# A two-layer attention kernel: feed-forward values held in PSUM from gate product to rounding, and the rounding offset made by two ScalarE passes

## The reference, cut to what matters

```python
def fp4_quant_dequant(x):                      # blocks of 16 along the last dim
    scale = max(abs(block)) / 6.0, at least 1e-12
    xn = xb / scale
    idx = searchsorted([0.25, 0.75, 1.25, 1.75, 2.5, 3.5, 5.0], abs(xn))
    q = [0, 0.5, 1, 1.5, 2, 3, 4, 6][idx] * sign(xn) * scale
def fp4_linear(x, w):
    return einsum('bsk,nk->bsn', fp4_quant_dequant(x), fp4_quant_dequant(w))
gate = fp4_linear(x, w_gate)                   # 128 -> 352
y = fp4_linear(x, w_up)
h = silu(gate) * y
return fp4_linear(h, w_down)                   # 352 -> 128, x is the layer-normalised input
```

## Time and profile before

| | us |
|---|---|
| median of 3 runs | 913.84 |
| lowest and highest of them | 913.34, 918.64 |
| the profiled execution, its own time | 913.45 |
| its span in the profile | 911.7 |
| first feed-forward step, first block maxima of x to last residual | 383.1 to 546.3 |
| second feed-forward step, the same | 745.4 to 909.0 |

### The profile page before, as it was taken

How to read it: one execution, slowest core, us unless ns; L and a number is a source line. 1 busy time by engine, 2 the same in 40 slices (tenths; PEclk the granted TensorE clock), 3 DMA queues, 4 the chain that set the end, 5 groups by cost and what they waited for, 6 DMA issues and landing times.

```text
span 911.7 us, 14036 instructions
## 1 busy us (share of the span) xinstructions
PE 639.3 (70%) x5231; PEld 464.9 (51%) x5231; DVE 584.0 (64%) x1062; ACT 300.4 (33%) x507; POOL 354.6 (39%) x423
## 2 busy tenths in 40 slices
PE   2458878887665777755766654899988965666575
PEld 1457756666333346734544442465555533554454
DVE  7525553331795985668988752566676657878863
ACT  2221113332242332044444321333333334444332
POOL 6620000000000001446777675255565444666664
PEclk9568999999897888968898966788999997889886
DMA  9300000000000000000000000000000000000001
GB/s 257 78 1 1 1 0 1 1 0 1 2 0 1 1 0 1 1 1 0 1 0 1 0 1 0 1 1 2 1 2 1 2 2 0 1 13 23 12 12 35
DMA packets 13676, 10.47 MB, mean 11 GB/s; under 512 B 1399, under 2 KB 12599, under 8 KB 13493
## 3 DMA queue, kind: packets, MB, share of 16 engines
q1 hardware_dynamic: 13620, 9.73, 3.8%
HBM read 7.63 MB, written 2.10 MB: 11 GB/s over the span
## 4 chain that ended last, share of the span: by engine, by line
PE 48%; DVE 23%; POOL 13%; issue 10%; ACT 5%; ACTq 0%; DMA 0%; DVEq 0%; POOLq 0%
PE ps L1052 5%; PE ps L1138 4%; PE ps L1270 4%; PE ps L1206 3%; PE ps L1167 3%; PE ps L1079 3%; PE ps L1188 3%; POOL arena L268 3%; PE ps L1289 2%; POOL arena L265 2%; DVE r L770 2%; POOL arena L258 2%; PE ps L1197 2%; DVE arena L845 2%; DVE hblk L818 2%
## 5 line engine op out<-in xcount | busy, mean ns | idle before, releaser
L1188 PE MATMUL ps<-wguT,arena 128*128 128x352 f32 x128 | 61.9, 572 | 34.5 <-DVE arena L845 33.1
L320 POOL TENSOR_TENSOR ln<-mv,lnc 128x4 f32<-128x4 f32 x64 | 13.6, 213 | 154.7 <-DVE mv L650 154.7
L339 POOL MEMSET early<- 128x2560 f32 x2 | 4.5, 2231 | 172.3 <-PE ps L1123 161.6
L1138 PE MATMUL ps<-G,xw 128*126 128x512 f32 x72 | 46.6, 800 | 30.0 <-ACT xw L492 22.3
L1180 PE MATMUL ps<-eye,arena 128*128 128x128 f32 x64 | 15.3, 383 | 73.7 <-POOL arena L258 65.3
L368 POOL TENSOR_SCALAR_AFFINE_SELECT arena<-arena 128x1024 f32<-128x1024 f32 x32 | 35.0, 1093 | 80.6 <-ACT arena L607 80.6
L1206 PEld LDWEIGHTS ps<-wdT,arena 128*128 128x128 f32 (+1 forms) x384 | 57.7, 226 | 15.2 <-ACT arena L546 7.6
L1206 PE MATMUL ps<-wdT,arena 128*128 128x128 f32 (+1 forms) x384 | 58.4, 311 | 5.4 <-ACT arena L546 5.4
L268 POOL TENSOR_TENSOR arena<-arena,hblk 128x704 f32<-128x704 f32 x32 | 60.1, 1880 | 2.5
L1189 PE MATMUL ps<-wguT,arena 128*128 128x352 f32 x128 | 57.1, 532 | 0.0
L931 DVE TENSOR_TENSOR arena<-ps,tri 128x1024 f32<-128x1024 f32 x32 | 39.2, 1224 | 27.2 <-PE ps L1270 27.2
(11 more groups left out here) (193 smaller groups left out, 1627.9 us busy)
## 6 DMA issues: line engine op xcount, KB each, us to landing
X<-in_x SPq DMA_DIRECT2D x8, 256.0 KB, 4.7
out<-X SPq DMA_DIRECT2D x8, 256.0 KB, 2.3
wqkv<-in_wqkv SPq DMA_DIRECT2D x1, 1024.0 KB
band<-in_band SPq DMA_DIRECT2D x1, 897.8 KB
early<-in_wfc SPq DMA_DIRECT2D x1, 512.0 KB
kI<-in_scaled_eye SPq DMA_DIRECT2D x1, 192.0 KB
wattn<-in_wattn SPq DMA_DIRECT2D x1, 192.0 KB, 7.5
S<-in_wd SPq DMA_DIRECT2D x1, 176.0 KB, 3.5
```

What stands on the lines that cost most here:

```text
L1138: last = mm(ps[0:WI, w, :], xw[:, w * WO:w * WO + WI], G1[:, b, :], start=True, stop=True)
L1188: mm(ps[:, 2 * k, 0:F], x, wguT[:, 0:F], start=True, stop=True).then_inc(s["f_gate"], 1)
```

## The change

The change does the following.

- h never goes to SBUF. Up lies in banks 1 and 2 for even pairs and 3 and 4 for odd ones (`up_banks`); `gated` multiplies in place, the maxima read there, the ratio is written there, and `move_h` reads there. All gate products share bank 0 (`GATE_BANK`), so a tile's gate waits for silu of the tile before.
- `normalise` writes x to PSUM bank 7 (`X_BANK`), where maxima and ratio work in place. That bank holds one quad, so normalise(q+1) waits until x(q) plus offset is done, where before it waited for the ratio.
- The offset is made by two ACT passes, `Square` (of 704 or 512 columns from PSUM, to bf16) and `Identity` with a bias of 2^22 * 4/3, in place of ACT's absolute value and DVE's clamp.
- Transposes of x and of h share bank 5 (`T_BANK`), and the second tile's transposes of h share bank 6 with down. `hT_copy` is two copies of 384 columns. For p = 1, DVE adds down from PSUM to X (`residual`), and neither `down_copy` nor POOL's residual is there.
- PE's `x_transposes` and ACT's `xT_copy` stand ahead of `gate_up(2r+3)` and `silu(2r+3)`. ACT's first `normalise` of p = 1 waits for the end of the linear attention.

```diff
+GATE_BANK, X_BANK, T_BANK = 0, 7, 5
+SQ = (RND / 6.0) ** 0.5
...
+            for k, c in enumerate((1e-5, -0.5, -1.0, RND * 4.0 / 3.0)):
...
-                    if 0 <= r - 3 < PN:
+                    if p == 0 and 0 <= r - 3 < PN:
                         residual(r - 3)
...
-                    need(a, "fx_ratio", n)
+                    need(a, "fx_moved", n)
...
+                def offset_h(r):
+                    n = ffn_pairs(p, r)
+                    a.wait_ge(s["fh_ratio"], n + 1)
+                    need(a, "fh_offset", n)
+                    act(hsquare[:, :].rearrange("p (k n) -> p k n", k=2), up_banks(r), ACT.Square, scale=SQ).then_inc(s["fh_square"], 1)
+                    a.wait_ge(s["fh_square"], n + 1)
+                    need(a, "fh_grid", n - 1)
+                    act(hoff[r % 2][:, :], hsquare[:, :], ACT.Identity, bias=lnc[:, 3:4]).then_inc(s["fh_offset"], 1)
...
                     if 0 <= r + 1 < PN:
                         silu(2 * r + 2)
-                    if 0 <= r - 2 < PN:
+                    if 0 <= r - 2 < PN and p == 0:
                         down_copy(r - 2)
+                    if r % 2 and q < QN:
+                        xT_copy(q)
                     if 0 <= r + 1 < PN:
                         silu(2 * r + 3)
                     if 0 <= r < PN:
-                        absolute("fh", hratio, hoff[r % 2], ffn_pairs(p, r), ffn_pairs(p, r) - 1)
+                        offset_h(r)
...
                         normalise(q + 1)
-                    if r % 2 and q < QN:
-                        xT_copy(q)
...
+                    up = up_banks(t // 2)[:, t % 2, :]
+                    tt(out=up, in0=up, in1=sil[t % 2], op=ALU.mult).then_inc(s["f_h"], 1)
...
+                def residual(r):
+                    v.wait_ge(s["f_down"], ffn_pairs(p, r + 1))
+                    tt(out=X[:, 2 * r:2 * r + 2, :], in0=ps[:, T_BANK + 1, 0:2 * P].rearrange("p (k c) -> p k c", k=2),
+                       in1=X[:, 2 * r:2 * r + 2, :], op=ALU.add).then_inc(s["f_x_done"], 1)
...
+                    need(pe, "f_silu", n)
+                    mm(ps[:, GATE_BANK, 0:F], x, wguT[:, 0:F], start=True, stop=True).then_inc(s["f_gate"], 1)
+                    need(pe, "fh_moved", ffn_pairs(p, max(r - 1, 0)))
+                    mm(up_banks(r)[:, t % 2, :], x, wguT[:, F:2 * F], start=True, stop=True).then_inc(s["f_up"], 1)
...
                         down_mms(r - 2)
+                    if r % 2 and q < QN:
+                        x_transposes(q, r)
                     if 0 <= r + 1 < PN:
                         gate_up(2 * r + 3)
-                    if r % 2 and q < QN:
-                        x_transposes(q)
                     if 0 <= r - 1 < PN:
                         h_transposes(r - 1)
```

More of the change, by code:

```diff
@@ L81, in build @@
         ln = sb("ln", [P, 4, TILES])
-        lnc = sb("lnc", [P, 3])
+        lnc = sb("lnc", [P, 4])
         rstd, shift = ln[:, 1, :], ln[:, 3, :]
@@ L102, in build @@
         used[0] = 0
-        xin, xratio, xmoved, xgrid = (part(QD * P) for _ in range(4))
+        xmoved, xgrid = (part(QD * P) for _ in range(2))
         xquant = part(QD * P).rearrange("p (k c) -> p k c", k=QD)
@@ L106, in build @@
         sil = [part(F) for _ in range(2)]
-        h, hratio, hgrid = (part(2 * F) for _ in range(3))
+        hgrid = part(2 * F)
         hmoved = [part(2 * F) for _ in range(2)]
@@ L551, in down_copy, with offset_x @@
                     need(a, "f_x_done", n - 1)
[L552 to L557, removed]
+                    act(down[r % 2], ps[:, T_BANK + 1, 0:2 * P].rearrange("p (k c) -> p k c", k=2), ACT.Copy).then_inc(s["f_down_copied"], 1)
+                def offset_x(q):
+                    n = ffn_quads(p, q)
+                    a.wait_ge(s["fx_ratio"], n + 1)
+                    need(a, "fx_offset", n)
+                    act(xsquare[:, :], ps[:, X_BANK, :], ACT.Square, scale=SQ).then_inc(s["fx_square"], 1)
+                    a.wait_ge(s["fx_square"], n + 1)
+                    need(a, "fx_grid", n)
+                    act(xoff[:, :], xsquare[:, :], ACT.Identity, bias=lnc[:, 3:4]).then_inc(s["fx_offset"], 1)
+                def offset_h(r):
[6 more added lines that the diff above has]
+                    act(hoff[r % 2][:, :], hsquare[:, :], ACT.Identity, bias=lnc[:, 3:4]).then_inc(s["fh_offset"], 1)
+                if p == 1:
+                    a.wait_ge(s["lin_x_done"], TILES)
                 normalise(0)
@@ L843, in gated, with absmax_h @@
                     v.wait_ge(s["f_up"], n + 1)
[L844 to L848, removed]
+                    up = up_banks(t // 2)[:, t % 2, :]
+                    tt(out=up, in0=up, in1=sil[t % 2], op=ALU.mult).then_inc(s["f_h"], 1)
+                def absmax_h(r):
+                    v.wait_ge(s["f_h"], ffn_tiles(p, 2 * r + 2))
+                    reduce(out=pair(hblk[r % 2][:, 0, :]), in_=blocks(up_banks(r)), axis=AX, op=ALU.max,
+                           apply_absolute_value=True).then_inc(s["fh_absmax"], 1)
@@ L862, in ffn @@
+                    if r % 2 == 0 and q < QN:
+                        absmax_x(q)
+                    if r % 2 and q < QN:
+                        move_x(q)
+                    if p == 1 and 0 <= r - 2 < PN:
+                        residual(r - 2)
+                    if 0 <= r < PN:
+                        inverse("fh", hblk[r % 2], ffn_pairs(p, r))
+                        ratio_h(r)
+                    if r % 2 == 0 and q < QN:
+                        ratio_x(q)
                     if p == 0 and 0 <= r - 4 < PN:
@@ L865, in ffn @@
                         tile_stats(2, 2 * r - 7)
[L866 to L878, removed]
+                    if 0 <= r < PN:
+                        move_h(r)
             ffn(0)
```

114 lines of the change are left out of this document (65 added, 49 removed).

## The result

| | before | after |
|---|---|---|
| median of four runs, us | 914.25 (913.34 to 918.64) | 943.01 (937.33 to 946.10) |
| the profiled execution's span | 911.7 | 944.4 |

The changed kernel is slower: ratio 1.0299, 95% interval 1.0242 to 1.0356. The forecast was 944.0, range 928 to 962.

A forecast was written before the change was run, and what follows sets the result against it. The prediction took a loop through several engines, with DVE close behind, as the bound. Per step 15.0 - 7.9 + 8.0 = 15.1, both 30.2, on 913.45 gave 943.7 and a median of 944; range 928 to 962.

The forecast's parts named there:

- Odd iterations: Feed-forward iterations in which x is rounded: gate and silu wait behind POOL's x, 13.0 us against 8.4 today.
- Even iterations: Feed-forward iterations between the odd ones: shorter way from ratio to addition, 7.5 us in place of 9.5 and more.
- 0.2 for DVE's residual: Even iterations: DVE's residual of p = 1 lies mostly under the wait for the scales and adds 0.2 us.
- The fill: First scale of x to gated of tile 1: 19.9 us where it was 12.0, 8.0 more per step.
- The new wait for the end of the linear attention: ACT's first normalise delayed by about 1 us, costed at nothing because POOL's first scale comes later anyway.
- Iterations without x and the tail: Iterations 12 to 14 at 6.35 us each save 5.9, the last iteration and behind it 2.0: -7.9 per step.
- rival C: Dearer: POOL's multiplies stay at 1.91 and 1.58, 957 us; or down at half clock in even iterations, 951; over 955: 0.16.
- A: Faster: contention goes and DVE's loop sets the pace everywhere, if x's transposes finish early; 850 us, chance 0.06.
- B: PE stays at 2.4 GHz, so transposes and gate save 0.9 per odd iteration: 932 us, chance 0.10.
- D: A wash: losses and gains cancel, needing odd iterations of 10.5 or less; about 915 us, chance 0.04.

The follow-up runs named there:

- e6: The changed kernel with x's transposes and their copy one iteration later, between down and gate of the even iteration: 854.0 us, ratio 0.9334.
- e8: The changed kernel with seven unused 128x352 matmuls on PE ahead of the wait for x in odd iterations 1 to 11: 933.9 us, ratio 1.0224.
- e3: The changed kernel with only ACT's copy of x moved behind silu(2r+3), ahead of the offset of h; PE as changed: 946.4 us, ratio 1.0335.
- e10: e6 with POOL making h's scale ahead of x's in even iterations and DVE's residual behind the ratio of h: 849.7 us, ratio 0.9305.
- e1: The changed kernel with PE's transposes of x and ACT's copy of x back at their places of before: 916.1 us, ratio 1.0018.
- e9: The kernel before with only x's transposes and their copy moved to the even iteration behind POOL's rounding of x: 901.6 us, ratio 0.9859.
- e5: The changed kernel with ACT's absolute value and DVE's clamp in place of Square and Identity: 936.2 us, ratio 1.0254.

## Why the prediction was right

**Odd iterations: 13.0 predicted, 12.95 measured.** Term by term in iteration 5 of the second step: start to scale 2.04 (2.03); to the subtraction 0.44 (0.43); to the multiply 1.59 (1.60); to PE's transposes 7.76 from the start (7.8); to gate 0.90 (0.86); to silu 1.42 (1.41); silu 0.36 (0.46); Square 0.78 and Identity 0.92 with their handovers (0.84 each); addition 0.81 (0.81). e6 shows that this order is what cost it: with nothing but the place moved, 12.95 becomes 6.34 to 7.65.

**Even iterations: 7.5 predicted, 7.33 and 7.38 measured.** Of the 0.2 for DVE's residual only 0.05 was there, the difference between the two steps: in iteration 6 it runs from 847.79 to 848.21, and the scale of h, for which the reciprocal waits anyway, is done at 848.04. Iterations 1 to 11 came to 114.4 per step instead of 115.5, +13.9 and not +15.0.

**The fill: +8.0 predicted, +8.0 measured** in both steps, and by the way that was laid out: in the second, x(0) takes from its scale at 764.47 to the transposes at 770.50 (6.0, predicted 5.9), normalise(1) starts at 772.12 behind the copy, and x(1) takes 6.0 again (774.61 to 780.58). The new wait for the end of the linear attention was put at nothing; POOL's first scale waited 0.18 us for the maxima behind it.

**Iterations without x and the tail: -7.9 per step predicted, -5.1 and -6.7 measured.** This is the mis-sized term. I gave all three iterations 6.35. Iterations 12 and 14 took 6.34 in the first step and 6.61 in the second, but iteration 13 took 7.74 and 8.25. So the three saved 4.0 and 3.6 and not 5.9. (In the first step they took 24.4 in the kernel before, where the prediction took 25.0 over from the second.) The last iteration and what is behind it saved 1.1 and 3.1 where I had 2.0 for both. Iteration 13 in the second step:

```profile
912.20 1.38 PE L1235 MATMUL ps<-wguT,arena 128*128 128x352 f32 x2
...
914.55 1.66 PE L1256 MATMUL ps<-wdT,arena 128*128 128x128 f32 x12
...
916.24 0.42 DVE L900 TENSOR_TENSOR X<-ps,X 128x256 f32<-128x256 f32 x1 [2.13 <-PE ps L1256]
...
916.58 0.42 DVE L848 RECIPROCAL hblk<-hblk 128x44 f32<-128x44 f32 x1
```

PE comes out of a thin stretch at half clock (gate and up 1.38 each), so down is late, DVE's residual waits for it for 2.13 us, and the reciprocal of h stands behind the residual although its scale was ready at 914.63. That is close to the mechanism that I had as half of rival C, and put into the even iterations instead; but down itself takes 1.66 here, and it is late because gate and up ran at half clock ahead of it. The first step has no residual on DVE. There gate and up take 1.36 and 1.38, down 2.03, and the gate behind them holds the silu that Square stands behind, 1.4 us after the ratio is done:

```profile
538.32 2.03 PE L1256 MATMUL ps<-wdT,arena 128*128 128x128 f32 x12
...
539.00 0.90 DVE L888 SCALAR_TENSOR_TENSOR ps<-ps,hblk 128x704 f32<-128x704 f32 x1
...
540.98 0.46 ACT L547 ACTIVATE arena<-ps 128x352 f32<-128x352 f32 x1 [0.21 <-PE ps L1235]
541.34 0.75 ACT L576 ACTIVATE hsquare<-ps 128x704 bf16<-128x704 f32 x1
```

In e8, where PE had been kept busy up to iteration 11, iteration 13 took 6.35 and 6.61, with gates of 0.76 in the second step. It is not there every time: e3, without that, took 7.73 and 6.61. So the term had left out that PE can come into an iteration without x at half clock.

**The sum.** Per step +13.9 + 8.0 - 5.9 = 16.0 against 15.1 predicted; the stages outside gave +0.6 net. The profiled execution took 946.1 instead of 943.7 and the median 943.0 instead of 944. The closeness of the last figure is in part luck: errors of opposite sign (-2.2 in the iterations, +4.0 in the tails), and a profiled execution that was the slowest of four between 937.3 and 946.1.

**The rivals.** *A* (850): the time of its world exists, e6 and e10, but needs the place that the change doesn't have; that condition was named. *B* (full clock): half clock was there, gate 1.38, and costs what B said, as e8 shows, 933.9 against B's 932. *C*: POOL's multiplies stayed at 1.38 and 1.06 throughout, so its first half is refuted; down took 1.60 in even iteration 6, so its second half did not come true where it was put. *D* (a wash) needed x two POOL instructions earlier; e1 gives 916 by another way, by moving the loss between iterations.

**The rule on DVE's fixed cost.** The Trainium skill (VectorE: DVE Perf Modes, section on the TRN2 errata) has a fixed cost that is 62 cycles higher for a PSUM source than for an SBUF one. The trace doesn't agree: the addition of h, with a PSUM source and its result in SBUF, takes 0.89 us, and the undisturbed one, all in SBUF, took 0.89 too. The ratio, PSUM to PSUM, takes 0.899 where the undisturbed one in SBUF took 0.89.

## What to carry to other kernels

When an edit shortens instructions on two busy engines, first find whom the last wait of the loop names; if it is a queue position on a third engine, the gain doesn't arrive until that position is changed too (here -1.4% for the place alone, +0.2% for the data alone, -6.7% for both). When an instruction consumes another engine's last result of an iteration, try it one iteration later, and not ahead of the work that this iteration needs; on PE and ACT, which run in the order of the code, that was worth 89 us here. Read the row of the consumer: an instruction that starts long after its data are there, and has no wait of its own, is held by its neighbour in the queue.

## What the runs showed of the hardware that I had not expected

- A clamp of 704 bf16 values with one SBUF source and one SBUF result on DVE took 0.97 us beside POOL's multiply and 0.33 alone. In e9 it took 0.86 beside POOL's residual. I had thought of the contention as one of two full SBUF inputs. The Trainium skill (GPSIMD Engine Reference, section Specifications) names two cases, DVE instructions with two SBUF inputs and those in a 2-port perf mode, and I had taken up only the first. The clamp has one SBUF input, so e5 and e9 agree with the page if it ran in such a mode, which no row shows.
- DVE writing its result to PSUM costs some 0.01 us more: the ratio took 0.899 us PSUM to PSUM where it took 0.891 in SBUF, and gated took 0.523 for 352 columns with its result in PSUM and 0.511 with it in SBUF.
- ACT's Identity from bf16 in SBUF to bf16 took 0.88 us for 704 columns, more than the absolute value of f32, 0.79, and than Square of f32 in PSUM, 0.76. Half the bytes bought nothing that shows. Identity also adds a bias read from a tensor, and no run here tells what of the 0.1 us is owed to that.
